# Sixteen-head local attention on one core: scores for eight heads in two banks, 32x32 turns on the Vector engine, one attend per sequence, a new order of the work

## The reference, cut to what matters

```
q, k, v = split(shift_tokens(x) @ Wqkv)          # 256 x 1024 each
q = q / |q| * q_scale ; k = k / |k| * k_scale    # norm of each head of each token
q = q*cos*scale + rotate_half(q)*sin*scale       # k likewise, with 1/scale
# window w of 32 queries sees the 64 keys of windows w-1 and w, with a mask
sim  = (q_w @ k_{w-1,w}.T) * 8 ; attn = softmax(mask(sim))
out  = attn @ v_{w-1,w}                          # 16 heads, 8 windows
x = out @ Wo + x
x = feed_forward(shift_tokens(x)) + x            # layer norm, W1 (a, gate), a*gelu(gate), W2
```

## Time and profile before

| | |
|---|---|
| three runs | 4221.27, 4227.32, 4227.56 us; median 4227.32 us |
| profiled execution, first to last instruction | 4218.7 us |
| mean granted TensorE clock | 0.987 |
| the transformer's full passes | from about 1065 us to about 4127 us |

### The profile page before, as it was taken

One profiled execution on the slowest core, in us unless ns is written; L12 is line 12 of the kernel. 1 busy time (PEld: TensorE's weight loads), 2 busy tenths in 40 slices (PEclk: granted clock), 3 DMA queues, 4 the chain that ended last, 5 costly groups with the idle time before them and its releaser, 6 DMA issues.

```text
span 4218.7 us, 144433 instructions
## 1 busy us (share of the span) xinstructions
PE 4055.8 (96%) x63591; PEld 2950.4 (70%) x63591; DVE 3292.4 (78%) x6966; ACT 2422.2 (57%) x4410; POOL 2231.4 (53%) x1352
## 2 busy tenths in 40 slices
PE   5999999887999999999999999999999999999997
PEld 4767777564777777777777777777777777777765
DVE  5345354457888988889888898888888888899995
ACT  3111101244767767667776677677667776776664
POOL 2010010025666666666666666666666666666663
PEclk8999999998999999999999999999999999999999
DMA  4111111001111111111111111111111111111110
GB/s 156 41 61 41 56 46 41 21 2 30 40 37 36 48 49 43 41 36 46 51 43 40 37 46 51 42 37 41 46 46 47 38 41 46 46 47 41 40 38 27
DMA packets 76614, 186.14 MB, mean 44 GB/s; under 512 B 16203, under 2 KB 45014, under 8 KB 71510
## 3 DMA queue, kind: packets, MB, share of 16 engines
q1 hardware_dynamic: 75254, 176.51, 13.6%
q10 hardware_dynamic: 736, 0.40, 0.0%
HBM read 61.25 MB, written 2.36 MB: 15 GB/s over the span
## 4 chain that ended last, share of the span: by engine, by line
PE 67%; DVE 5%; ACT 3%; issue 1%; POOL 1%; DMA 0%; POOLq 0%; DVEq 0%; SPq 0%
PE pQ L1690 15%; PE pTO L1723 9%; PE pS L1674 9%; PE pM L1758 7%; PE pM L1747 7%; PE pTO L1736 7%; PE pC L1792 6%; PE pTO L1704 3%; PE pC L1802 3%; ACT sq L1555 2%; ACT pS L1539 1%; DVE rot L1404 1%; DVE m L1408 1%; DVE n L1419 1%; POOL rot L1322 1%
## 5 line engine op out<-in xcount | busy, mean ns | idle before, releaser
L1322 POOL TENSOR_TENSOR rot<-rot,m 128x1024 f32<-128x1024 f32 x384 | 906.4, 2360 | 385.7 <-DVE m L1408 385.7
L1314 POOL TENSOR_TENSOR rot<-rot,rn 128x1024 f32<-128x1024 f32 x384 | 733.7, 1911 | 280.6 <-DVE rn L102 280.6
L1555 ACT ACTIVATE sq<-pQ 128x1024 f32<-128x1024 f32 x380 | 390.1, 1027 | 437.0 <-PE pQ L1690 436.8
L1331 POOL TENSOR_TENSOR E<-E,rc 128x512 f32<-128x512 f32 x384 | 401.2, 1045 | 346.0 <-DVE rc L1394 345.7
L1723 PEld LDWEIGHTS pTO<-PT,V 64*64 64x64 f32 x24576 | 401.5, 134 | 108.9 <-issue 100.2
L1404 DVE TENSOR_TENSOR rot<-pQ,tabl 128x1024 f32<-128x1024 f32 x380 | 456.9, 1202 | 12.1 <-ACT sq L1555 10.0
L1408 DVE TENSOR_TENSOR m<-pQ,tabl 128x1024 f32<-128x1024 f32 x380 | 461.4, 1214 | 0.0
L1419 DVE TENSOR_REDUCE n<-sq 128x16 f32<-128x1024 f32 x380 | 459.3, 1209 | 0.0
L1674 PEld LDWEIGHTS pS<-kT,qT 64*32 64x32 f32 x24576 | 360.9, 107 | 136.6 <-issue 101.7
L1723 PE MATMUL pTO<-PT,V 64*64 64x32 f32 x24576 | 443.5, 221 | 4.3 <-ACT PT L1564 2.8
L1674 PE MATMUL pS<-kT,qT 64*32 64x64 f32 x24576 | 424.9, 218 | 21.9 <-issue 12.5
(11 more groups left out here) (231 smaller groups left out, 6939.8 us busy)
## 6 DMA issues: line engine op xcount, KB each, us to landing
V<-V SPq DMA_DIRECT2D x192, 384.0 KB, 3.5
b_cB<-b_crow SPq DMA_DIRECT2D x32, 1024.0 KB, 5.9
xs<-XT SPq DMA_DIRECT2D x192, 64.0 KB, 2.9
V<-V SPq DMA_DIRECT2D x96, 128.0 KB, 3.3
ys<-XT SPq DMA_DIRECT2D x192, 64.0 KB, 2.0
wq<-in_wqkv SPq DMA_DIRECT2D x6, 512.0 KB, 4.4
wk<-in_wqkv SPq DMA_DIRECT2D x6, 512.0 KB, 4.2
wv<-in_wqkv SPq DMA_DIRECT2D x6, 512.0 KB, 5.4
```

The source lines that it names most:

```text
L1314: e.tensor_tensor(r, r, rn[b % 2][:, c:c + HEADS].unsqueeze(2).to_broadcast([P, HEADS, HD]), ALU.mult)\
L1322: e.tensor_tensor(rot[j % RING][:, :], rot[j % RING][:, :], m2[:, :, :].rearrange("p h d -> p (h d)"), ALU.add)\
```

## The change

- The mask is written to a [128, 2x512] area (`pS` is now two banks): `scores` works on eight heads per call, two calls per item instead of four, 64 small matmuls each. Head pair s of a column of heads j uses rows 64*s, columns 32*j and bank s. `less_max`, `exponent`, `sums` and `by_sum` work on 128x1024, twice per item.
- `probs` moves from PE and ACT to DVE: one `transpose` of 128x1024 per call (each 32x32 block turned in place), twice per item, straight into `PT`; PE's 16 transposes per item and ACT's four copies are gone.
- v is computed window by window onto 32 partitions for each j (`values`: four calls, each 8 matmuls of 32 weight columns by 256 streamed, at columns 32*j). The three DMAs that shifted v are gone.
- `attend` is one call per item with 128 matmuls: contraction 32 keys, 64 columns, 64 queries streamed (32 in the last window), rows 32*j, columns 64*s, row group j into bank j of a new four-bank area `pW`, added up over the two windows of keys. `pW` holds `pS`, `pO` and `pM[1]` at other times. `heads_out` copies two banks per call, twice.
- `roots` is gone from DVE: POOL takes the maximum and the half (`norms_half`), ACT makes ln and exp(-0.5 ln) (`norm_log`, `norm_root`, 128x64 each), POOL does one Newton round of four operations (`newton`). ACT loads one table with both ln and exp after the last gelu, so there are still two table loads per item.
- `turn` and `turned` work on halves, in an order with the values; all five lists of calls have a new order, as has SP's.

```
-            def probs(n, g):                      # PE
-                for b in range(4):
-                    x = e.transpose(pT[:, b * P:(b + 1) * P], E[i % 2][:, b * P:(b + 1) * P], ident[:, :])
+            def probs(n, g):                      # DVE
+                e.wait_ge(g_no.sem, g_no.at("no", 2 * n + g))
+                if n:
+                    e.wait_ge(p_pv.sem, p_pv.at("pv", n - 1))
+                e.transpose(PT[:, g, :, :].rearrange("p s k -> p (s k)"), E[g][:, :]).then_inc(v_tt.sem, 1)

 scores, PE
-                for b, w in enumerate(ORDER):
+                for w in range(NW):
                     for j in range(4):
-                        x = e.matmul(pS[32 * j:32 * j + 32, b * KEYS:(b + 1) * KEYS], ..., tile_position=(r, 32 * j))
+                        for s in range(2):
+                            x = e.matmul(pS[32 * j:32 * j + 32, s * 512 + w * KEYS:s * 512 + (w + 1) * KEYS],
+                                         q[HD * s:HD * s + HD, 4 * g + j, WIN * w:WIN * (w + 1)],
+                                         k[HD * s:HD * s + HD, 4 * g + j, WIN * w:WIN * (w + 2)], ...,
+                                         tile_position=(HD * s, 32 * j))

+            def attend(n):                        # PE
+                if n:
+                    e.wait_ge(v_wo.sem, v_wo.at("xa", n - 1))
+                e.wait_ge(a_v.sem, a_v.passed(n + 1))
+                e.wait_ge(v_tt.sem, v_tt.at("tt", 2 * n + 1))
+                if n + 1 < NP:
+                    e.wait_ge(v_s.sem, v_s.at("su", 2 * n + 3))
+                free(1)
+                at_rest(e)
+                for v in range(NW):
+                    wd = KEYS if v < NW - 1 else WIN
+                    for g in range(2):
+                        for j in range(4):
+                            for s in range(2):
+                                x = e.matmul(pW[HD * s:HD * s + HD, 512 * j + L * g + WIN * v:512 * j + L * g + WIN * v + wd],
+                                             V[n % NB][32 * j:32 * j + 32, v, P * g + HD * s:P * g + HD * s + HD],
+                                             PT[32 * j:32 * j + 32, g, s, (2 * v + 1) * WIN:(2 * v + 1) * WIN + wd],
+                                             start=(v == 0 and g == 0), stop=(v == NW - 1 and g == 1), skip_group_check=True,
+                                             tile_position=(32 * j, HD * s))

+            def values(n, k):                     # PE
+                for i in range(2):
+                    for j in range(4):
+                        x = e.matmul(pM[b][32 * j:32 * j + 32, L * i:L * (i + 1)], xs[n % 3][:, WIN * (2 * k + i):WIN * (2 * k + i + 1)],
+                                     wv[:, :, P * j:P * (j + 1)], start=True, stop=True, tile_position=(0, 32 * j))
```

More of the change, by code:

```diff
@@ L1143, in transformer_phase @@
     RING = 5
+    NB = 3
+    HG = N // 2
+    LIFT = 16
+    GROUPS = 2 * NW
+    MOVES = "v0 v1 t0b t0a v2 t1a v3 t1b t2a t2b t3b t3a".split()
+    side = {m: i % 2 for i, m in enumerate(MOVES)}
     with ctx:
@@ L1366, in tables @@
             def tables(n):
+                if n is None or not starts(n):
+                    return
                 l = n // NSEQ
@@ L1492, in _ @@
             for A, R, B, Dn, C, F in passes():
-                if A is not None and starts(A):
-                    tables(A)
+                tables(A)
                 less_max(B, 0)
+                cosines(A, 0)
+                sines(A, 0)
                 statistics(C)
-                rotate(A, 0)
+                squares(A, 0)
                 normal(C)
-                squares(A, 0)
+                squares(A, 1)
+                cosines(A, 1)
+                sines(A, 1)
                 less_max(B, 1)
                 sums(B, 0)
-                rotate(A, 1)
-                squares(A, 1)
-                roots(A if A is not None else NP if R == NP - 1 else None)
                 last_stats(F)
-                attention_add(Dn)
-                less_max(B, 2)
-                sums(B, 1)
-                hidden(C, 0)
-                rotate(A, 2)
-                less_max(B, 3)
-                squares(A, 2)
-                last_normal(F)
-                sums(B, 2)
-                hidden(C, 1)
-                hidden(C, 2)
-                sums(B, 3)
-                rotate(A, 3)
+                cosines(A, 2)
+                hidden(C, 0)
+                sines(A, 2)
+                squares(A, 2)
+                sums(B, 1)
+                last_normal(F)
+                probs(B, 0)
+                squares(A, 3)
+                hidden(C, 2)
+                cosines(A, 3)
+                sines(A, 3)
+                probs(B, 1)
+                hidden(C, 1)
+                attention_add(Dn)
                 ffn_add(C)
-                squares(A, 3)
         @block.scalar
@@ L1817, in _ @@
                 project(A, 0)
+                values(R, 0)
+                values(R, 1)
+                turn(R, "0b")
+                turn(R, "0a")
                 back(C)
-                probs(Dn, 3)
-                turn(R, 0)
+                project(A, 1)
+                values(R, 2)
+                turn(R, "1a")
+                normed(C)
                 scores(B, 1)
-                attend(Dn, 3)
-                project(A, 1)
-                values(R, 0)
-                normed(C)
-                combine(Dn)
-                probs(B, 0)
+                values(R, 3)
                 hidden(C, 0)
                 last(F)
+                turn(R, "1b")
                 project(A, 2)
-                scores(B, 2)
-                turn(R, 1)
+                turn(R, "2a")
                 hidden(C, 1)
-                attend(B, 0)
-                turn(R, 2)
-                scores(B, 3)
-                probs(B, 1)
-                values(R, 1)
+                attend(Dn)
+                hidden(C, 2)
                 project(A, 3)
-                hidden(C, 2)
-                attend(B, 1)
-                turn(R, 3)
-                probs(B, 2)
+                turn(R, "2b")
+                combine(Dn)
+                turn(R, "3b")
+                turn(R, "3a")
                 contract(C)
-                attend(B, 2)
 def layout(i):
```

393 lines of the change are left out of this document (194 added, 199 removed).

## The result

The changed kernel takes 4522.98 us (median of 4 runs, 4516.96 to 4531.21), the kernel before 4225.47 us (4 runs): ratio 1.071, 95% interval 1.0695 to 1.0725. I had forecast 4116 us, in a range from 3970 to 4300. The kernel is 7% slower, and the forecast has the wrong sign.

The account below looks back on a forecast made before the run. PE was taken to bound the kernel at 32.98 us a pass; afterwards PE's sum 29.2 plus waits set by order gives 31.66. 92 passes save 121 us, wv costs 10: 4227 - 121 + 10 = 4116 us, range 3970 to 4300.

Parts of the forecast that it names:

- PE's own sum: PE's work per pass after the change: 33.0 us less probs, scores and attend savings, plus values, gives 29.2.
- rival 2: PE can't be fed faster than a pair in 14.7 ns; scores 1.92 us, pass 33.2, 4257 us; chance 0.22.
- Order and tail: In the pass, DVE's work after project(A,3) makes PE's contract wait 1.5 us; small waits precede project(A,1) and turn "2a".
- Scores: On PE, 128 pairs on eight places side by side take 1.03 us a call, two calls 2.06 instead of 4.12.
- Attend: On PE, 3.9 us an item instead of 4.3: loads onto one column half follow each other, streams on different rows overlap.
- Values: On PE, four rounds make 1.0 us a call; four calls 3.9 us instead of 3.4.
- Transposes: The two new transposes on DVE cost 1.2 us, as every 1024 operation of DVE.
- rival 4: DVE's transposes wait for POOL as the first of roots does; pass 32.1 to 34.4, middle 4266 us; chance 0.08.
- wv: SP issues the next layer's wv behind fetch_ys, so PE's values wait two us at five layer changes: 10 us.
- Rival 3: Matmuls on different rows of the same columns don't run side by side: attend 7.3, pass 36.6, about 4570 us; chance 0.15.
- Rival 1: Loads onto different rows overlap in attend on PE: attend 2.0, pass 30.3, 3991 us; chance 0.13.

Follow-up runs that it names:

- e4: Changed kernel with attend in two halves of 128 pairs, hidden(C,2) and project(A,3) between them, and hidden(C,1) early on DVE: 4158.6 us, ratio 0.9845.
- e5: Changed kernel with 32 columns streamed instead of 64 by every matmul of scores and attend, as many instructions: 4572.9 us (one run).
- e8: e6 with SP issuing the next layer's wv ahead of fetch_ys instead of behind it: 4248.2 us, ratio 1.0052 to the kernel before.
- e10: e4 with SP issuing the next layer's wv ahead of fetch_ys: 4141.7 us, ratio 0.9803 to the kernel before.
- e3: Changed kernel with attend in two halves of 128 pairs, hidden(C,2) and project(A,3) between them, and some turns and ACT calls reordered: 4240.3 us, ratio 1.0042.
- e1: Changed kernel with attend taking only key windows 0, 2, 4, 6, so 128 pairs in one run instead of 256: 4154.6 us, ratio 0.9836.
- e6: e4 with hidden(C,1) and hidden(C,2) between attend's halves, project(A,3) behind, and ACT's heads_out ahead of square(A,3): 4265.7 us, ratio 1.0096.

## Why the prediction was wrong

The step that failed is PE's own sum: it priced the pairs of scores and attend by streaming and loads alone and put the supply of PE with instructions at nothing. I took a run of pairs to go on for as long as its call is, and dismissed rival 2 with "the gaps in the timeline are fully explained by streaming". That was true of the earlier trace rows, where runs are 64 pairs or 128 (scores and attend together), just a block. The change puts four runs of 64 pairs into one of 256, and there PE stands: 204.5 us in attend and 34.2 in scores.

The trace of the kernel before had a sign, in its waits of PE (1065 to 4127):

```profile
PE pS L1674 <- issue: 12.5, 13, 1.3
```

Each of these 13 waits at the old scores ends 1.2 to 1.5 us after a packet of instructions has landed, as the gaps of the changed kernel do. The last column of the earlier trace rows, 100.2 us of idle of the loads ended by "issue", is no such sign: in the full passes these are 276 idles of some 0.34 us, three a pass, while PE itself was busy.

A pass was forecast at 31.66 and came to 36.5. Of the 4.8 us between, 2.7 are the gaps, 1.0 is PE's own work (29.2 forecast; 30.2 measured, in e4's pass less its waits: scores 0.8 more, the projections 0.4 more, attend 0.9 less, all the rest 0.6 more), about 1.3 is what is left for the lower clock, and the other waits were 0.2 less than forecast.

Point by point:

- **Order and tail.** Contract's wait for DVE's hidden(C,1): forecast 1.5, measured 163.4 us over 91 waits, 1.8. The idle of DVE ahead of squares(A,3) and its releaser were right as well; it was longer wherever attend stood (362.4 us in all, forecast 1.5 a pass). The small waits ahead of project(A,1) and turn "2a" were not there in this pass; 0.22 stood ahead of turn "0a", for ACT's V.
- **Scores.** Forecast 1.03 a call, measured 1.41 where no gap breaks it: too little by 0.4, 0.8 a pass. The bound is no longer streaming but some 5 ns an instruction (e5). The Trainium skill, "TensorE: Matmul & The Clock Gate", section "Measured speedup vs the span model", has about 4 ns for issuing one more tile. By the trace it is 10.0 for a pair of load and matmul.
- **Attend.** Forecast 3.9. By speed it is 2.7 (256 pairs at 10.6 ns), 3.0 as two calls from start to start in e4: the 3.9 came from loads on one half of the columns following each other at 0.0293 us, and they do not (the earlier trace rows did not show what I read from it). The Trainium skill, "TensorE: Matmul & The Clock Gate", part 3, has weight loads overlap with running matmuls of other row groups; the trace agrees, with 2.7 us for what would be 3.9 if they did not. With its pauses attend is 5.4 from first to last pair.
- **Clock.** I forecast none of it. PE's own 30.2 us, 2.7 of gaps, 1.8 at contract and 0.5 of small waits a pass come to 35.2; the 1.3 up to 36.5 are what is left for the lower clock, some 115 us in all. That is a remainder; the fit's 0.41 x 3.0 gives about as much. The Trainium skill, "TensorE: Matmul & The Clock Gate", section "A second HAM failure mode: psum-queue depth-cycling", says that short idles between groups of matmuls can make the clock swing. The trace agrees, with pauses of 1.1 and 2.2 us ahead of its fall (3218.8 to 3225.1 us above).
- **Values** 1.0 a call (3209.80 to 3210.80), as forecast. **Transposes** on DVE 1.23, forecast 1.2, so rival 4 falls:

```profile
3236.03 1.24 DVE L1419 STREAM_TRANSPOSE PT<-E 128x1024 f32<-128x1024 f32 x1
3237.19 0.44 DVE L1484 SCALAR_TENSOR_TENSOR hh<-pC,vec,hh 128x256 f32<-128x256 f32 x1
```

- **wv.** Forecast 10 us, measured 4.6 of PE's waits in the changed kernel; in the quicker orders the edit of SP's list gave 17 (e8, e10).
- **The rivals.** Rival 3 (4570 us) came nearest to the time by a mechanism that is false: the row groups run side by side. Rival 2 had the right place, the feed of PE, but as a rate (14.7 ns a pair, where PE takes 10.0), not as blocks with a latency; it gave 4257. Rival 1 was right that loads on different rows overlap, but attend's speed was 2.7, not 2.0. None was the case.

Open: what exactly lowers the clock. In the changed kernel 58 of 61 stretches at half clock begin in or just behind a gap of attend, and they are gone with the gaps in e3 and e4. But falls come at PE's waits for DVE as well (25 of 30 in e1), e5 has it lower with about the same gaps, and e6 with a wait for DVE between the halves.

## What to carry to other kernels

Count instructions and not only columns: in these traces a run of small matmuls longer than a block of 256 instructions (128 pairs of load and matmul) starves, as a block has to have some 3.45 us of work in it before the next is ready, so set long matmuls between short bursts. When many small calls are merged into one, look in the profile of before at the waits of PE itself (not of its loads) that "issue" ends, and at what the merged run will be next to. After a merge, redo the order: here the halved attend, one call of DVE and one load of SP moved ahead, and a projection around the second half turned +7% into -3.6%.

## What the runs showed of the hardware that was not expected

- PE's instructions come in packets of 16 KB on a DMA queue of their own, one at a time (532 packets, none overlaps another): about 3.45 us from the entry into one block to the readiness of the next, 1.4 of it after the packet has landed (1.2 to 1.6 in the 131 gaps of attend).
- A pair of load and matmul on eight places takes 10.0 ns from start to start (32 weight columns, 64 streamed; 1.27 us from the first of 128 matmuls to the last), and 8.6 with half the columns streamed (e5).
- Pauses inside a burst of small matmuls often cost again behind it, at a granted clock of 0.50. In the full passes of the changed kernel a stretch at half clock followed 34 of the 35 attends with two pauses and 26 of the 57 with one; of 91 calls of project(A,3) 54 took over 1.95 us from start to start, instead of 1.7 to 1.8, and 18 over 3.2.
